# Two-layer Mamba, expert, global and local attention kernel: a new instruction order from a corrected table-load charge, and one exponential a block with a VectorE sum in the last two pairs

## The chip, the cores and the metric

The kernel runs on one core of a Trainium2 chip. The metric is the device time of one execution in microseconds (us), as the median of several runs; lower is better.

## The reference, cut to what matters

The input is `x` of shape (16, 256, 128). Layer 0 adds a Mamba block and a mixture of experts to the normalized input; layer 1 adds two things to it: a global attention and two layers of a local (windowed) attention with a feed-forward part. The change touches the global attention, and, through the order, everything else. Its core is:

```python
q, k, v = _l2norm(q), _l2norm(k), v           # 16 heads of 8
cos = einsum('bhsd,bhtd->bhst', q, k)
g_dist = arccos(clip(cos, -1 + 1e-7, 1 - 1e-7))
attn_score = (1.0 + g_dist) ** (-3.2)
n_r = sum(attn_score, axis=-1)
n_c = sum(attn_score, axis=-2)
k_tilde = n_r ** -1 * attn_score * n_c ** -1
probs = k_tilde / maximum(sum(k_tilde, axis=-1), 1e-12)
out = einsum('bhst,bhtd->bhsd', probs, v)
```

## The kernel before, in words

The 16 sequences of 256 tokens go in 8 pairs (numbers 0 to 7). All work is cut into units: `e_*` are those of the experts (early in the program), `m_*` those of the Mamba scan, `f_*` the normalization between the layers, `g_*` the global attention, and the names in `LAYER` (shift, qkv, norm, heads, score, pt, rsum, pv, on, wo, ln, up, gelu, hid, down) the local attention and its feed-forward part, two layers for each sequence of a pair. A unit has one to four stages, each on one engine.

**What sets the order.** Nothing is left to chance at run time: `schedule()` (from L449) simulates the program on the host before the kernel is built, with a table of durations (`STAGES`, `durations`), a constant `LOAD_TIME` of 1.29 for a change of ScalarE's function table, and for each unit a wanted time. The wanted times come from a rough layout of the pairs plus two tables of offsets, `LATER` (one number for a kind of unit) and `STREAM` (one for each pair of each kind of work). At each moment an engine takes, of the units that are ready, the one with the smallest wanted time; on ScalarE, a unit that needs another table than the loaded one counts 127 later. The result is one list of units for each of TensorE, ScalarE, VectorE, GpSimd and SyncE, and the engines run these lists in order, waiting on semaphores for each other. So a change of the tables changes the order on every engine, and nothing that is computed.

**Table changes.** Ln and Exp share one table, Tanh and Arctan (`g_tan`) need the sigmoid table, Gelu and Silu have their own; Tanh alone is also run with the gelu or silu table. `use()` (L840 to L846, the load is L844) issues one load where the loaded table isn't among those that serve. The planner charges a `g_tan` that comes from the Ln and Exp table with two loads (L529), the kernel issues one there.

**The global attention.** For each sequence of a pair the 16 heads are done in 4 blocks of 4 heads, so a pair has 8 blocks. Block m works in the buffers `cl[m % 2]` and `la[m % 2]`, each 128 x 2048 in SBUF (4 heads, 2 halves of the keys, 256 queries), and `vt[m % 2]`:

- `g_score`: TensorE makes the cosines (L1093), VectorE clips them into `cl` (L1652)
- `g_ln`: ScalarE takes two logarithms (L1390, L1392); `g_sub`: GpSimd subtracts them (L1855)
- `g_tan`: Tanh and Arctan (L1398, L1401), each one instruction of 128 x 2048
- `g_pow`: one Ln of 128 x 2048 (L1408), then eight Exp of 128 x 256 (L1413), one for each head and half, each of which also adds its own row up and writes the sum to `vt` (the profile shows the read of the accumulator as an instruction of its own at L1413)
- `g_av`: VectorE takes the reciprocal of these sums (L1661) and scales the values (L1664), TensorE multiplies (L1107); after every second block ScalarE copies the product (L1422)

The logarithm of block m + 2 waits for the product and for the scaled values of block m, as they use the same buffers. A unit of the local attention that VectorE shares with these is the negated maximum of its scores (L1729); its qkv unit sums squares with a reduction of 128 x 1024 to 128 x 16 (L1704); ScalarE's exponential there is L1465, its copy of q and k L1457, and its square of q and k L1439.

Of the kernel before, what the change touches and what calls it, by code (L numbers as in the profile page):

```python
# [6 lines left out]
ALU = mybir.AluOpType  # L7
ACT = mybir.ActivationFunctionType
AX = mybir.AxisListType
# [25 lines left out]
GH, GD = 16, 8  # L35
HB = 4
# [46 lines left out]
LOAD_TIME = 1.29  # L83
# [6 lines left out]
         "norm": "ln", "pt": "ln", "rsum": "ln", "ln": "ln", "m_in": "silu", "g_tan": "tan", "gelu": "gelu"}  # L90
SWITCH = 127.0

LATER = {"down": 17.13, "e_down": 0.92, "e_lg": -1373.3, "e_ln": 621.99, "e_load": -1698.97, "e_place": -129.783, "e_pre": 351.489,
         "e_route": 144.702, "e_scat": 829.618, "e_store": -223.789, "e_tr": -184.595, "e_up": 44.242, "e_xn": -28.591, "e_xt": -830.714,
         "f_ln": 818.98, "f_tr": -1660.36, "f_xn": -118.536, "f_yg": -111.816, "g_av": 89.144, "g_avT": -202.085, "g_ev": -784.392,
         "g_hd": -35.958, "g_ln": 938.103, "g_norm": -59.145, "g_oT": 238.89, "g_out": 718.35, "g_pow": 876.48, "g_qkv": 45.815,
         "g_score": 49.652, "g_sq": 72.566, "g_sub": 570.978, "g_tan": 44.449, "gelu": -343.785, "heads": 43.677, "hid": -127.469,
         "l_weights": 625.975, "ln": -124.928, "ln2": 1.634, "lnT": -15.963, "m_B": -153.424, "m_C": 17.261, "m_bx": 50.752,
         "m_dt": 18.917, "m_du": 21.175, "m_ex": -16.259, "m_fin": 74.245, "m_hc": 137.244, "m_in": -23.847, "m_load": -295.604,
         "m_out": -935.123, "m_scan": 731.575, "m_sum": 14.942, "m_turn": -247.837, "m_weights": -173.243, "m_xp": 895.808,  # L100
         "norm": -15.561, "on": -140.182, "out": 284.565, "pt": -39.622, "pv": 82.873, "qkv": 47.209, "qn": -65.566, "rsum": -2.347,
         "score": -4.24, "shift": -70.641, "up": -71.786, "wo": 25.239, "x_load": 44.744}

STREAM = {("-", 0): 147.932, ("e", 0): -62.078, ("e", 1): 166.105, ("e", 2): -162.027, ("e", 3): 122.427, ("e", 4): 496.972, ("e", 5): -233.745,
# [14 lines left out]

LOADED = [15.0, 24.0]  # L120

# [7 lines left out]


BY_HALF = 2


def step_of(n, k):
# [30 lines left out]
def durations(unit):  # L165
    u, n, b, k = unit
    if u == "e_xt" and n >= GJ[1]:
        return [("PE", 0.11), ("DVE", 0.22)]
    if u == "e_up" and n >= GJ[1]:
        return [("PE", 0.89), ("DVE", 0.82)]  # L170
    if u == "m_in":
        return [("PE", 0.86), ("ACT", 0.62)] if k % 2 else [("PE", 0.86), ("DVE", 3.15), ("ACT", 0.62)]
    if u == "e_scat":
        return [("POOL", 1.5 * TT * (GP[n + 1] - GP[n]))]
    if u == "qkv":
        return [("PE", 0.86), ("ACT", 0.6)] if k % 3 else [("PE", 1.72), ("ACT", 1.02), ("DVE", 3.6), ("POOL", 2.36)]
    return STAGES[u]
# [253 lines left out]
def schedule():  # L431
# [13 lines left out]
    table = "ln"  # L445
# [50 lines left out]
    while done < todo:  # L496
        for x in [y for y in waiting if y[0] <= now]:
            waiting.remove(x)
            offer(x[1], 0, now)
        again = True  # L500
        while again:
            again = False
            for e in engines:
                if free_at[e] > now:
                    continue
                best = None
                for x in engines[e]:
                    unit, stage, _ = x
                    if not may(unit, stage):
                        continue  # L510
                    needs = NEEDS.get(unit[0]) if e == "ACT" else None
                    cost = want[unit] + (SWITCH if needs and needs != table else 0)
                    if best is None or cost < best[0]:
                        best = (cost, x, needs)
                if best is None:
                    continue
                unit, stage, _ = x = best[1]
                engines[e].remove(x)
                taken.update(holds(unit)[0].get(stage, []))
                needs_banks = takes_banks(unit)  # L520
                if needs_banks and needs_banks[0] == stage:
                    banks[bank_of(unit)] = choose(unit, needs_banks[1])
                    for m, z in enumerate(banks[bank_of(unit)]):
                        idle.remove(z)
                        before_it[bank_of(unit), m] = held_by.get(z)
                        held_by[z] = (bank_of(unit), m)
                takes = stages(unit)[stage][1]
                if best[2] and best[2] != table:
                    takes += LOAD_TIME * (2 if best[2] == "tan" and table == "ln" else 1)  # L529
                    table = best[2]  # L530
                if e == "DVE" and unit[0] in DUAL:
                    takes += max(0.0, pool_until - now)
                    dual_until = now + takes
                if e == "POOL" and unit[0] in POOLED:
                    takes += max(0.0, dual_until - now)
                    pool_until = now + takes
                free_at[e] = now + takes
                plan[e].append(unit)
                line(unit, e).pop(0)
                events.append((now + takes + lands(unit, e), done, unit, stage))  # L540
                done += 1
                again = True
        times = [x for x in free_at.values() if x > now] + [x[0] for x in events + waiting]
        if not times:
            raise ValueError([(e, x[:3]) for e, x in engines.items()])
        now = min(times)
        for x in sorted(y for y in events if y[0] <= now):
            events.remove(x)
            finish(x[2], x[3], x[0])
# [31 lines left out]
def build(nc, d, out):  # L581
    ctx = ExitStack()
    with ctx:
# [160 lines left out]
        for x_, y_ in ((a0, a0), (a2, a3)):  # L744
            q = len(wE)
# [525 lines left out]
        def scalar_program():  # L1271
            for u, i, b, k in order(plan, "ACT"):
# [130 lines left out]
                elif u == "g_pow":  # L1403
# [3 lines left out]
                    a.wait_ge(a_own, arctan_done[m])  # L1407
                    a.activation(at, at, ACT.Ln, bias=one_b[:, 1:2], scale=-2.0).then_inc(a_own, na.up())  # L1408
                    a.wait_ge(a_own, na.n)
                    for hi in range(HB):  # L1410
                        for kt in range(2):
                            part = at[:, hi, kt * L:(kt + 1) * L]
                            e = a.activation(part, part, ACT.Exp, scale=-3.2, accum_out=vt[m % 2][:, kt, hi, GD + 2:GD + 3])  # L1413
# [74 lines left out]
        def vector_program():  # L1488
            for u, i, b, k in order(plan, "DVE"):
# [164 lines left out]
                elif u == "g_av":  # L1654
# [3 lines left out]
                    if m >= 2:  # L1658
                        v.wait_ge(p_av, m - 1)
                    w = vt[m % 2]  # L1660
                    v.reciprocal(w[:, :, :, GD], w[:, :, :, GD + 2]).then_inc(v_own, nv.up())  # L1661
                    v.wait_ge(v_own, nv.n)
                    for kt in range(2):
# [374 lines left out]
```

## Time and profile before

| | us |
|---|---|
| median of 3 runs (2258.05 to 2261.52) | 2261.49 |
| the profiled execution | 2262.57 |
| its span, first to last instruction | 2261.3 |
| busy: PE, DVE, ACT, POOL | 1788.6, 1697.8, 1739.7, 541.0 |

The profile is that of one execution. PE is TensorE, PEld its weight loads, DVE VectorE, ACT ScalarE, POOL GpSimd, SP SyncE. A group of instructions is named by its line in the kernel; "ACT_TABLE_LOAD" at L844 is a load of ScalarE's table. The chain of waits is followed back from the last instruction, at each step to what released it, and ends where it can't be followed; here it covers the span from 1908 us on.

### The profile page before, as it was taken

Reading aid. Unit: us, or ns where it says so; the run is one execution under the profiler, and the core shown is the slowest. Engines: PE = TensorE matmul, PEld = TensorE weight load, DVE = VectorE, ACT = ScalarE, POOL = GpSimd, SP = SyncE. Lnnn points to the kernel's source line nnn. Section 1 sums busy time; section 2 is a strip of 40 time slices with the busy share of each in tenths; the row PEclk is TensorE's granted clock in tenths of the full one; section 3 lists DMA queues with packets and bytes.
Section 4 is the critical chain, followed back from the end, with each engine's and each line's share of the span. In section 5 each row is a group of like instructions: output and inputs, shape, how many; then the busy total and the mean of one; then the engine's idle time right before and its main releaser. Section 6 shows DMA issues by size and latency. Waiting matters only on the chain. (4 is left out here: it accounts for less than half of the span.)

```text
span 2261.3 us, 40539 instructions
## 1 busy us (share of the span) xinstructions
PE 1788.6 (79%) x15282; PEld 1293.3 (57%) x15282; DVE 1697.8 (75%) x2517; ACT 1739.7 (77%) x2887; POOL 541.0 (24%) x270
## 2 busy tenths in 40 slices
PE   3668788998778977788688887886778786779787
PEld 2654566776466654555465565554556464556565
DVE  4878887775999698859976889749984799655552
ACT  2435786857888697887878988977589958887996
POOL 2231122222311222312232222302142121232230
PEclk9687778999889888898788887998988888889888
DMA  6751214350341133114310233013300242000000
GB/s 227 237 170 48 71 38 135 117 147 18 127 136 52 53 117 108 43 39 131 113 39 14 73 122 103 10 49 121 130 21 2 84 141 84 1 1 2 6 1 6
DMA packets 81651, 177.39 MB, mean 78 GB/s; under 512 B 10388, under 2 KB 41940, under 8 KB 81332
## 3 DMA queue, kind: packets, MB, share of 16 engines
q1 hardware_dynamic: 75632, 163.53, 22.4%
q0 software_dynamic: 2816, 7.21, 1.0%
q10 hardware_dynamic: 3012, 4.06, 0.5%
q8 instruction: 125, 2.05, 0.4%
q14 instruction: 66, 0.54, 0.1%
HBM read 161.92 MB, written 12.85 MB: 77 GB/s over the span
## 5 line engine op out<-in xcount | busy, mean ns | idle before, releaser
L1855 POOL TENSOR_TENSOR arena<-arena 128x1024 f32<-128x1024 f32 x128 | 316.3, 2493 | 622.8 <-ACT arena L1392 622.6
L1859 POOL TENSOR_TENSOR arena<-arena,rb 128x1024 f32<-128x1024 f32 x64 | 152.2, 2378 | 866.5 <-DVE rb L1711 866.5
L1579 DVE TENSOR_TENSOR_SCAN ps<-dA,ps 128x1024 f32<-128x1024 f32 x128 | 291.0, 2284 | 1.6 <-ACT dA L1351 1.0
L1153 PE MATMUL ps<-w_l_wqkv,arena 128*128 128x512 f32 x384 | 205.8, 670 | 23.0 <-DVE hB L1587 6.4
L844 ACT ACT_TABLE_LOAD x153 | 196.3, 1283 | 19.3 <-issue 16.6
L1413 ACT ACTIVATE arena<-arena 128x256 f32<-128x256 f32 x512 | 205.3, 402 | 2.0
L1351 ACT ACTIVATE dA<-mv,w_A_log 128x510 f32<-128x510 f32 x256 | 167.8, 711 | 42.2 <-DVE ps L1579 39.1
L1093 PE MATMUL ps<-gqT,gkT 8*128 8x256 f32 x1024 | 164.7, 460 | 38.9 <-DVE arena L1652 16.1
L1652 DVE TENSOR_SCALAR arena<-ps 128x1024 f32<-128x1024 f32 x128 | 155.0, 1217 | 51.3 <-PE ps L1093 50.7
L1573 DVE TENSOR_TENSOR ps<-BC,mv 128x1024 f32<-128x1024 f32 x128 | 181.6, 1425 | 12.9 <-ACT arena L1457 4.1
L849 PE MATMUL ps<-w_ident,arena 128*128 128x128 f32 x623 | 112.1, 326 | 99.5 <-DVE arena L1512 28.6
L1043 PE MATMUL ps<-w_ident,hB 128*128 128x128 f32 x1024 | 162.4, 312 | 28.7 <-DVE hB L1587 28.6
L1043 PEld LDWEIGHTS ps<-w_ident,hB 128*128 128x128 f32 x1024 | 136.5, 162 | 54.4 <-DVE hB L1587 33.2
L1729 DVE TENSOR_REDUCE nmx<-ps 128x4 f32<-128x512 f32 x128 | 87.8, 686 | 97.8 <-PE ps L1181 97.2
L849 PEld LDWEIGHTS ps<-w_ident,arena 128*128 128x128 f32 x623 | 87.2, 169 | 125.0 <-issue 83.2
L1587 DVE TENSOR_TENSOR hB<-ps,BC 128x1024 f32<-128x1024 f32 x128 | 154.4, 1214 | 4.4 <-PE ps L1043 3.6
L1093 PEld LDWEIGHTS ps<-gqT,gkT 8*128 8x128 f32 x1024 | 101.0, 213 | 80.4 <-issue 70.4
L1192 PE MATMUL ps<-arena 64*128 64x192 f32 (+1 forms) x1024 | 118.5, 352 | 35.1 <-DVE rb L1711 13.9
L1390 ACT ACTIVATE arena<-arena,one_b 128x2048 f32<-128x2048 f32 x64 | 127.7, 1996 | 22.8 <-DVE arena L1652 20.9
L1192 PEld LDWEIGHTS ps<-arena 64*128 64x128 f32 x1024 | 92.5, 207 | 83.8 <-issue 49.9
L1153 PEld LDWEIGHTS ps<-w_l_wqkv,arena 128*128 128x128 f32 x384 | 74.4, 211 | 101.9 <-issue 94.1
L1392 ACT ACTIVATE arena<-arena,one_b 128x2048 f32<-128x2048 f32 x64 | 128.2, 2003 | 2.1
(223 smaller groups left out, 4507.7 us busy)
## 6 DMA issues: line engine op xcount, KB each, us to landing
BC<-bc_d SPq DMA_DIRECT2D x224, 512.0 KB, 4.2
BC<-in_experts SPq DMA_DIRECT2D x16, 514.0 KB
arena<-in_experts SPq DMA_DIRECT2D x15, 514.0 KB
mv<-in_experts SPq DMA_DIRECT2D x15, 514.0 KB, 3.4
arena<-in_x SPq DMA_DIRECT2D x8, 256.0 KB, 4.7
xnT_d<-arena SPq DMA_DIRECT2D x8, 256.0 KB, 3.0
hB<-xnT_d SPq DMA_DIRECT2D x8, 256.0 KB, 2.6
x<-in_x SPq DMA_DIRECT2D x8, 256.0 KB, 5.6
```

The costliest lines, as they stand in the source:

```text
L844: a.preload_act_table_set(names[0])
L849: return t.transpose(out_, in_, ident[0:k, 0:k])
L1043: e = t.matmul(lb()[:, tt * P:(tt + 1) * P], hB[k % 2][:, j, tt * P:(tt + 1) * P], ident, is_transpose=True, start=q == j == tt == 0, stop ...
L1093: e = t.matmul(lb(z)[:, kt * L:(kt + 1) * L], gkT[32 * hi:32 * hi + GD, hb, kt * P:(kt + 1) * P], gqT[32 * hi:32 * hi + GD, hb], start=Tru ...
L1153: e = t.matmul(lb(z), hT1[b][:, tt * P:(tt + 1) * P], w_lqkv[:, l, (w + z) * INNER:(w + z + 1) * INNER], start=True, stop=True)
L1192: t.matmul(lb(z)[:, cols], kT[head_rows(z), k, at:at + P], qT[head_rows(z), k, at:at + cols.stop - cols.start], start=kt == 0, stop=False)
L1351: e = a.activation(dA[k % 2][:, j].rearrange("p (s l) -> p s l", s=2)[:, :, 1:], dtv[:, c].rearrange("p (s l) -> p s l", s=2)[:, :, 1:], A ...
L1413: e = a.activation(part, part, ACT.Exp, scale=-3.2, accum_out=vt[m % 2][:, kt, hi, GD + 2:GD + 3])
L1573: v.tensor_tensor(two_banks(unit), Bb[j % 2], bc(du[:, c:c + 1], [P, NG, T]), ALU.mult).then_inc(v_bx, 1)
L1579: v.tensor_tensor_scan(h_, flat2(dA[k % 2]), h_, 0.0, ALU.mult, ALU.add).then_inc(v_scan, 1)
L1652: v.tensor_scalar(cl[m % 2][:, 2 * (k % 2):2 * (k % 2) + 2], two_banks(unit), -1.0 + 1e-7, 1.0 - 1e-7, ALU.max, ALU.min).then_inc(v_gs, 1)
L1855: g.tensor_tensor(la[m % 2][:, half], la[m % 2][:, half], cl[m % 2][:, half], ALU.subtract).then_inc(g_sub, 1)
```

## The change

Five edits. The numbers of `LATER` and `STREAM` are replaced, all of them, so the order on every engine is another. The planner charges one load for each change of table. A constant `LATE = 6` is added: in pairs 6 and 7 `g_pow` issues a single Exp of 128 x 2048 without row sums, and `g_av` on VectorE begins with one reduction that adds up the 256 queries for each key, half and head (2048 elements a partition to 8), with a semaphore wait behind it. The planner's durations for these two units follow. Pairs 0 to 5 keep the eight Exp.

```diff
-LATER = {"down": 17.13, "e_down": 0.92, "e_lg": -1373.3, ...
+LATER = {"down": 21.789, "e_down": -179.804, "e_lg": 315.988, ...
-STREAM = {("-", 0): 147.932, ("e", 0): -62.078, ("e", 1): 166.105, ...
+STREAM = {("-", 0): 145.797, ("e", 0): -176.079, ("e", 1): -91.561, ...
...
 BY_HALF = 2
+LATE = 6
...
+    if u == "g_pow" and n >= LATE:
+        return [("ACT", 4.05)]
+    if u == "g_av" and n >= LATE:
+        return [("DVE", 2.75), ("PE", 1.0)]
...
                 if best[2] and best[2] != table:
-                    takes += LOAD_TIME * (2 if best[2] == "tan" and table == "ln" else 1)
+                    takes += LOAD_TIME
                     table = best[2]
...
                     a.activation(at, at, ACT.Ln, bias=one_b[:, 1:2], scale=-2.0).then_inc(a_own, na.up())
                     a.wait_ge(a_own, na.n)
-                    for hi in range(HB):
+                    if i >= LATE:
+                        e = a.activation(at, at, ACT.Exp, scale=-3.2)
+                    for hi in range(HB if i < LATE else 0):
                         for kt in range(2):
                             part = at[:, hi, kt * L:(kt + 1) * L]
                             e = a.activation(part, part, ACT.Exp, scale=-3.2, accum_out=vt[m % 2][:, kt, hi, GD + 2:GD + 3])
                     e.then_inc(a_at, 1)
...
                     w = vt[m % 2]
+                    if i >= LATE:
+                        v.tensor_reduce(w[:, :, :, GD + 2], la[m % 2].rearrange("p h (k q) -> p k h q", k=2), AX.X, ALU.add).then_inc(v_own, nv.up())
+                        v.wait_ge(v_own, nv.n)
                     v.reciprocal(w[:, :, :, GD], w[:, :, :, GD + 2]).then_inc(v_own, nv.up())
```

Of the wanted times, the ones of the global and local attention and of the scan move little: `g_pow` 876.48 to 816.827, `g_score` 49.652 to 53.464, `score` -4.24 to -2.312, `STREAM` of ("g", 7) -130.691 to -139.982, of ("l", 7) -214.869 to -198.142. The experts' and single others move by hundreds.

## Rows read from the trace of the kernel before

**Rows 1.** The page, part 1: busy time, share of the span and instructions.

```profile
PE 1788.6 (79%) x15282; PEld 1293.3 (57%) x15282; DVE 1697.8 (75%) x2517; ACT 1739.7 (77%) x2887; POOL 541.0 (24%) x270
```

**Rows 2.** Busy time by stretch; columns: length, PE, PEld, DVE, ACT, POOL, clock, DMA.

```profile
1867.00:1940.00 73.00, 50.63 (x440) 35.69 (x444) 59.80 (x73) 65.34 (x120) 16.09 (x7) 0.84 0.20 66
...
1940.00:2262.00 322.00, 257.77 (x2498) 186.38 (x2489) 161.76 (x299) 267.32 (x443) 81.66 (x34) 0.87 0.01 3
```

**Rows 3.** The chain that ended last: shares of the span by engine, then by line.

```profile
PE 6%; ACT 6%; DVE 2%; issue 1%; DVEq 0%; ACTq 0%
...
by line: ACT arena L1413 1.2%; ACT L844 1.1%; issue 1.0%; PE ps L1234 0.8%; PE ps L849 0.8%; ACT arena L1408 0.8%; PE ps L1153 0.7%; ACT arena L1398 0.7%; PE ps L1093 0.5%; ACT arena L1401 0.4%; PE ps L1192 0.4%; PE ps L1107 0.4%; PE ps L12
```

**Rows 4.** Groups of instructions on ACT, whole span.

```profile
L1413 ACT ACTIVATE arena<-arena 128x256 f32<-128x256 f32 x512 | 205.3, 402 | 2.0
...
L1408 ACT ACTIVATE arena<-arena,one_b 128x2048 f32<-128x2048 f32 x64 | 127.5, 1992 | 0.0
...
L1413 ACT ACTIVATION_READ_ACCUMULATOR arena<-arena 128x1 f32 x512 | 95.4, 186 | 0.0
```

**Rows 5.** Groups on ACT from 1867 to 2262 us, where pairs 6 and 7 take powers.

```profile
L1413 ACT ACTIVATE arena<-arena 128x256 f32<-128x256 f32 x128 | 51.3, 402 | 0.5
L844 ACT ACT_TABLE_LOAD x32 | 41.1, 1283 | 0.6
```

**Rows 6.** The chain in order of time; columns: start, length, what.

```profile
1983.00 0.18 ACT arena L1413
1983.19 0.59 ACT arena L1465
...
2143.66 2.19 ACT arena L1413 x11
...
2146.51 1.93 PE ps L1107 x16
...
2227.55 3.31 ACT arena L1413 x16
...
2230.88 0.22 DVE vt L1661
...
2231.67 1.93 PE ps L1107 x16
```

**Rows 7.** Groups of instructions on DVE, whole span: the kernel's reductions.

```profile
L1729 DVE TENSOR_REDUCE nmx<-ps 128x4 f32<-128x512 f32 x128 | 87.8, 686 | 97.8 <-PE ps L1181 97.2
L1704 DVE TENSOR_REDUCE lss<-arena 128x16 f32<-128x1024 f32 x64 | 77.5, 1210 | 53.0 <-ACT arena L1439 52.9
```

**Rows 8.** Waits from 1940 to 2262 us: total, times, longest.

```profile
DVE vt L1661 <- ACT arena L1413: 19.5, 6, 4.5
...
PE ps L1107 <- DVE vt L1664: 3.9, 2, 2.4
```

**Rows 9.** ACT in order of time: first and last of 35 loads straight before Tanh (L1398).

```profile
245.51 1.33 ACT L1351 ACTIVATE dA<-mv,w_A_log 128x510 f32<-128x510 f32 x2 [1.46 <-DVE ps L1579]
246.86 1.28 ACT L844 ACT_TABLE_LOAD   x1
248.15 1.91 ACT L1398 ACTIVATE arena<-arena 128x2048 f32<-128x2048 f32 x1
...
2217.74 0.70 ACT L1465 ACTIVATE arena<-ps 128x640 f32<-128x640 f32 x1
2218.46 1.28 ACT L844 ACT_TABLE_LOAD   x1
2219.76 1.91 ACT L1398 ACTIVATE arena<-arena 128x2048 f32<-128x2048 f32 x1
```

**Rows 10.** The page, part 5: all table loads.

```profile
L844 ACT ACT_TABLE_LOAD x153 | 196.3, 1283 | 19.3 <-issue 16.6
```

**Rows 11.** L844 in two stretches of 180 us; columns: length, ACT busy, clock, DMA.

```profile
820.00:1000.00 180.00, 19.25 (x15) 0.89 0.18 61
1000.00:1180.00 180.00, 10.26 (x8) 0.85 0.30 98
```

More of the change, by code:

```diff
@@ L91 @@
 SWITCH = 127.0
[L93 to L102, printed above, removed]
@@ L104 @@
-STREAM = {("-", 0): 147.932, ("e", 0): -62.078, ("e", 1): 166.105, ("e", 2): -162.027, ("e", 3): 122.427, ("e", 4): 496.972, ("e", 5): -233.745,
[14 rows of a table removed]
+LATER = {"down": 21.789, "e_down": -179.804, "e_lg": 315.988, "e_ln": 174.252, "e_load": -80.536, "e_place": -412.31, "e_pre": 197.091,
+         "e_route": -422.17, "e_scat": 75.416, "e_store": 746.088, "e_tr": 28.199, "e_up": 22.441, "e_xn": -25.847, "e_xt": -1283.66,
+         "f_ln": 932.194, "f_tr": -415.066, "f_xn": -136.104, "f_yg": 296.043, "g_av": 87.191, "g_avT": -1295.52, "g_ev": -639.753,
+         "g_hd": -34.805, "g_ln": 1296.35, "g_norm": -166.971, "g_oT": 533.127, "g_out": 372.703, "g_pow": 816.827, "g_qkv": 41.118,
+         "g_score": 53.464, "g_sq": 26.042, "g_sub": 80.328, "g_tan": 55.828, "gelu": -375.199, "heads": 50.829, "hid": -644.16,
+         "l_weights": 372.755, "ln": -519.782, "ln2": 3.395, "lnT": -0.939, "m_B": 443.054, "m_C": 126.829, "m_bx": 155.512,
+         "m_dt": 46.846, "m_du": 38.48, "m_ex": -12.305, "m_fin": 234.25, "m_hc": 183.447, "m_in": -28.599, "m_load": 252.041,
+         "m_out": -1249.76, "m_scan": 584.13, "m_sum": 17.216, "m_turn": -660.129, "m_weights": -235.564, "m_xp": 1282.27,
+         "norm": -23.494, "on": -821.145, "out": 329.735, "pt": -24.861, "pv": 81.567, "qkv": 47.234, "qn": -624.114, "rsum": 3.63,
+         "score": -2.312, "shift": -80.128, "up": -44.353, "wo": 27.438, "x_load": -205.723}
@@ L120 @@
+STREAM = {("-", 0): 145.797, ("e", 0): -176.079, ("e", 1): -91.561, ("e", 2): -22.018, ("e", 3): -92.228, ("e", 4): -49.362, ("e", 5): -706.602,
[14 rows of a table added]
 LOADED = [15.0, 24.0]
```

28 rows, old and new, of the table STREAM are left out of this document.

## The prediction

> **What bounds the kernel now.** I read the page's busy shares first. PE, ACT and DVE are all busy for 75 to 79% of the span [rows 1]: no engine is full, and what is lost is lost in hand-overs between three nearly equal engines. So work taken from one engine comes back only in part, and the place decides how much. The power step of pairs 6 and 7 (the last 16 of 64 blocks) lies between 1867 and 2262 us, where 128 of the 512 small Exp stand [rows 5]. Next, busy time by stretch: from 1867 to 1940 us DVE is busy 59.80 of 73.00 us beside ACT's 65.34; the Mamba scan still runs there. From 1940 us on, DVE is busy only 161.76 of 322.00 us, PE 257.77, ACT 267.32, so ACT is the fullest at 83% [rows 2]. That is where 12 of the 16 blocks lie (96 of the 128 Exp). Last, the chain of waits: of the span PE and ACT have 6% each, DVE 2%, and the line with the largest share is L1413 itself with 1.2%, or 27 us; the table loads have 1.1% [rows 3]. The change works on the two largest single lines of the end.
>
> **The change, part by part.** The sum is made against the profiled execution, 2262.57 us (span 2261.3 and 1.27 around it); it lies 1.08 above the median, 2261.49, so 1.08 comes off at the end.
>
> Part 1, **the single Exp.** Eight Exp with their reads of the accumulator take 3.31 us in a row [rows 6]; 8 x 0.402 + 8 x 0.186 would be 4.70, so the reads mostly overlap the next Exp [rows 4], and only the stretch in the chain is a fair price. One instruction of 128 x 2048 without a pointer for its bias takes 1.91 us [rows 9], with one 1.99 [rows 4]. The new Exp has none, so 1.91 and a saving of 1.40 a block (1.32 if it is the other). For 16 blocks: 22.4 us of ACT, 16.8 of them after 1940 us.
>
> Part 2, **the reduction.** The kernel has reductions of 512 and 1024 elements a partition, 0.686 and 1.210 us [rows 7]. The step is 0.524 for 512 more, so 2048 takes 1.210 + 2 x 0.524 = 2.26 us. The bounds are 2.26 and 4 x 0.686 = 2.74; the larger row is the nearer, and it reads SBUF as the new one does, so 2.26. For 16 blocks 36.2 us of DVE. It starts when the whole Exp is done, as the reciprocal L1661 did, so the path from the Ln's end to the first product L1107 grows by 2.26 - 1.40 = 0.86 us a block, and 0.05 for the wait. Before, reciprocal and scaling took from 2230.88 to 2231.67 [rows 6]. Room on DVE: 13.20 us idle up to 1940, 160.24 after [rows 2]. The four early blocks ask for 9.0 of the 13.2: no room worth the name. The twelve late ones ask for 27.1 of 160.24. Behind the waiting g_av on DVE stand the clip L1652, the maximum L1729 and the local layers' other steps; TensorE waits for these, and the logarithm of the block after next waits for the product and the values. DVE already waits at L1661 for L1413 six times after 1940, 19.5 us in all; with the Exp 1.40 earlier that shrinks by up to 8 us, which pays for part of the reduction [rows 8].
>
> What of this is on the path? L1413's 27 us in the chain are 27 / 3.31 = 8.2 blocks. Most of these go on with other ACT work, as at 1983.00 to 1983.19; two go over to the product, at 2143.66 and at 2227.55 [rows 6]. The first kind gains 1.40, the second loses 0.91: 6.2 x 1.40 - 2 x 0.91 = 6.9 us. That is the low bound, since other blocks are off this chain only by a little. The high bound is all 22.4. Between them: the tail as a share of ACT's load, 16.8 x 0.83 = 13.9, nothing for the four early blocks, where DVE's 9.0 us more stand against ACT's 5.6 less, and about 2 off for the two hand-overs. I take **-12**. If the cover of DVE's idle time were gone, each reduction would cost its full 2.26.
>
> Part 3, **the planner's charge.** 35 of the 153 loads stand straight before Tanh after work of the Ln and Exp table, at 246.86 the first and at 2218.46 the last [rows 9, 10]. Before, each was charged twice, 35 x 1.29 = 45 us of ScalarE time that the plan held and the chip never spent. The chip didn't pay it, so removing it saves nothing by itself. What it can bring is an order in which the other engines' work is ready when ScalarE really is.
>
> Part 4, **the new order.** The trace can't price an order that it doesn't hold. The bounds come from the table loads: two stretches of 180 us have 15 and 8 loads, 19.25 and 10.26 us [rows 11]; the mean is 153 x 180 / 2261 = 12.2. If all the kernel were like the sparser, 4.2 x 12.6 = 53 fewer loads, 68 us of ACT; like the denser, 2.8 x 12.6 = 35 more, 45 us. By ACT's share of the chain, 6 of 15, that is -27 to +18. Neither end is likely: the last pairs already stand at 32 loads for 16 blocks, 2.0 a block against 153 / 64 = 2.4 for the whole [rows 5, 10]. The wanted times that place scan, scores and powers barely move, so the large layout stays, and experts, whose numbers move by hundreds, come early beside other work. I take **-4**, some eight loads fewer or as much idle time, as a plan with the right charge should fit better than one with 45 us too many; there is no row for more. The SyncE and GpSimd queues are reordered too: POOL is busy 24% [rows 1], and a DMA issued later would show as a wait of DVE or PE in the scan. I cost it at nothing, covered by the prefetch of two buffers; without the cover it would be a few us a pair and is inside the bounds.
>
> Weighed against a rule: before and after the loads ACT loses 0.02 us or less: 245.51 + 1.33 = 246.84, load at 246.86, done at 248.14, Tanh at 248.15; the same at 2218.46 [rows 9]. So a switch costs 1.30 here, and a single charge of 1.29 is right. The Trainium skill, "ScalarE: Activation LUTs", section "What ACT_TABLE_LOAD costs", has every switch at about 2.66 us, a load of 1.28 and a drain of 1.38; the load agrees, the drain isn't seen in these rows. By the page the old double charge of 2.58 would be the right one and the repair a mistake.
>
> Sum: -12 - 4 = -16; 2262.57 - 16 = 2246.6, less 1.08 is **2245.5 us**.
>
> **The rivals.** (A) The forecast, 0.52: 2245, own range 2230 to 2256.
> (B) The order is worth more, 0.12: the loads fall toward the sparser stretch and half of the 27 comes; 2261.5 - 12 - 16 = about 2233 and below, down to 2220. For it: 35 double charges spread over the whole kernel, and 40 us and more of each engine idle in every 180. Against: hand-overs and not loads hold most of that.
> (C) No change, 0.17: PE, 80% busy in the tail and with as much of the chain as ACT, closes the gap; only the 6.9 of the low bound comes, and 4 are lost in a less lucky order; 2258.6.
> (D) Slower by the reduction, 0.10: the product waits for it in most blocks, because the local layers' steps stand before g_av in DVE's new list or because PE has nothing else. A block whose product is on the path loses 0.91; all 16 on it: 14.6, 2276. The others gain 12 / 14 = 0.86 each by my sum (two of 16 hand over today), so it decides from 0.91 n = 0.86 (16 - n), eight blocks. For it: those two in the chain [rows 6]. Against: PE waited only twice, 3.9 us, for the scaled values [rows 8], and DVE is idle for half of the tail.
> (E) Slower by more loads, 0.07: a cheaper charge lets the plan switch oftener. Toward the denser stretch, 35 more, +18 against -12: 2267.5. It decides from 12 / (1.30 x 0.4) = 23 more loads.
> (F) The repair is a mistake, 0.02: if a switch had a cost as long again as the load itself, the plan would now be short by 45 us of ScalarE time and the others' work early and in the way; by the share of 0.4 +18, less 12: 2267.5. This is what the page's 2.66 us comes to. The rows with 0.02 us on both sides of a load leave it little.
> That the new order doesn't do what it is planned for is in C and E.
>
> **How the numbers follow.** The likeliest case gives 2245.5. Range 2223 to 2269: it holds A and C whole, most of B, and of the slow cases what isn't near the bound of D; some 2 in 10 stay out. About 0.2% (4.5 us) is what a measurement of this kernel can tell from none. Faster, below 2257: A, B and a little less, 0.63. Same: most of C and the edge of A, 0.18. Slower, above 2266: D, E, F, 0.19.
>
> **What would show it.** Part 1: at L1413 384 small Exp and 16 of 128 x 2048 at 1.91 us. Part 2: 16 reductions of 128 x 2048 at about 2.26 us on DVE, and L1661 waiting for ACT less than 19.5 us in the tail. Part 3 and 4: table loads near 145 instead of 153, still with 0.02 us before and after; ACT busy about 1707 in place of 1739.7 and DVE about 1734. The end of the scan (L1579) should stay within some us of where it is, with the gain after it. The forecast is wrong if PE's waits at L1107 for the scaled values or at L1093 grow by over 10 us in the tail, if the loads rise, or if the time before 1867 us changes by more than 10 us either way: then the order, and not the single Exp, made the result.

## The result and the profile after

The changed kernel takes 2191.56 us (median of 4 runs, 2180.23 to 2203.48) against 2261.27 for the kernel before on the same chip; the ratio is 0.9696, 95% interval 0.9643 to 0.9748. That is 70 us or 3.0% less, against 16 forecast, and under the range's low end of 2223. The profiled execution took 2192.96 us, its span 2191.6.

The page of the changed kernel, part 1 and the first line of part 4 (as rows 1 and 3 of before):

```profile
PE 1763.4 (80%) x15282; PEld 1279.0 (58%) x15282; DVE 1729.8 (79%) x2533; ACT 1712.0 (78%) x2644; POOL 536.2 (24%) x270
...
PE 6%; ACT 3%; DVE 2%; issue 2%; DVEq 0%; ACTq 0%
```

The busy times are the forecast ones: ACT 1712.0 (forecast 1707, before 1739.7), DVE 1729.8 (forecast 1734, before 1697.8) [rows 1]. The work is what it was said to be, yet the span is 70 us shorter. So the gain is mostly idle time that is gone, on every engine. ACT and DVE together have even a little more to do than before (3441.8 against 3437.5). PE did the same 15282 matmuls in 25 us less, at a mean granted clock of 0.870 against 0.863. The clock doesn't make the gain: where both kernels ran beside each other (e9 below), the kernel before took 2259.20 us at 0.869, and the changed one 2188.44 at 0.870.

Groups of the changed kernel on DVE and ACT: the reduction, the single Exp, the small Exp that are left, the table loads:

```profile
L1669 DVE TENSOR_REDUCE vt<-arena 128x8 f32<-128x2048 f32 x16 | 36.4, 2278 | 9.7 <-ACT arena L1416 9.7
```

```profile
L1420 ACT ACTIVATE arena<-arena 128x256 f32<-128x256 f32 x384 | 154.0, 402 | 1.5
...
L1416 ACT ACTIVATE arena<-arena 128x2048 f32<-128x2048 f32 x16 | 30.6, 1911 | 0.5
```

```profile
L849 ACT ACT_TABLE_LOAD x150 | 192.4, 1283 | 17.2 <-issue 14.5
```

The reduction takes 2.278 us where 2.26 was worked out [rows 7], the Exp 1.911. The loads are 150, three fewer than the 153 of [rows 10].

The time comes from the order, and shows in how much is done by the end of the scan. The scan's last instruction begins at 1910.7 us before and at 1913.2 after. Busy time up to its end and behind it; columns as in rows 2. The kernel before:

```profile
0.00:1913.40 1913.40, 1508.99 (x12620) 1093.12 (x12620) 1521.32 (x2200) 1452.64 (x2399) 453.58 (x234) 0.86 0.29 92
1913.40:2261.40 348.00, 279.58 (x2662) 200.21 (x2662) 176.48 (x318) 287.08 (x488) 87.41 (x36) 0.86 0.01 3
```

The changed kernel:

```profile
0.00:1915.40 1915.40, 1533.23 (x13022) 1114.30 (x13022) 1552.04 (x2258) 1512.54 (x2424) 475.29 (x244) 0.87 0.28 92
1915.40:2191.70 276.30, 230.13 (x2260) 164.65 (x2260) 177.80 (x277) 199.50 (x221) 60.91 (x26) 0.88 0.01 3
```

In the same 1914 us the changed order gets 60 us more of ACT's work and 402 more of PE's matmuls done beside the scan. What is left for the end, where DVE has little to do, falls from 348 to 276 us. ACT's own saving behind the scan can't make that: it is at most 16 x 1.40 = 22 us in all. An order can gain at another place, too: e7 below does it by an earlier end of the scan.

### The profile page after: what moved, and what is told of

The parts are those of the page before. It is cut to its first block and busy times, and to the rows that moved or that the text cites. A ratio compares the mean times of both kernels' runs of the same rounds, so it can differ in the third digit from the quotient of the medians.

```text
span 2191.6 us, 40312 instructions
## 1 busy us (share of the span) xinstructions
PE 1763.4 (80%) x15282; PEld 1279.0 (58%) x15282; DVE 1729.8 (79%) x2533; ACT 1712.0 (78%) x2644; POOL 536.2 (24%) x270
## 5 line engine op out<-in xcount | busy, mean ns | idle before, releaser
L1580 DVE TENSOR_TENSOR ps<-BC,mv 128x1024 f32<-128x1024 f32 x128 | 188.4, 1477 | 8.1 <-ACT arena L1472 1.9
L1420 ACT ACTIVATE arena<-arena 128x256 f32<-128x256 f32 x384 | 154.0, 402 | 1.5
```

The costliest lines, as they stand in the source:

```text
L1580: v.tensor_tensor(two_banks(unit), Bb[j % 2], bc(du[:, c:c + 1], [P, NG, T]), ALU.mult).then_inc(v_bx, 1)
```

## The experiments

All ratios are to the kernel before, run beside each kernel on the same chip. The experiments ran in three groups, and its median differed between them: 2244.4 us for e1 to e4, 2250.7 for e5 to e8, 2265.0 for e9 to e12. The first expectations are in us beside the 2261 of the first result; where a median and a ratio say different things, the ratio counts.

### The four corners: which part made it

**e1_exps_old_order.** The kernel before, every engine's list as it was; the planner isn't touched.

```diff
+LATE = 6
...
-                    for hi in range(HB):
+                    if i >= LATE:
+                        e = a.activation(at, at, ACT.Exp, scale=-3.2)
+                    for hi in range(HB if i < LATE else 0):
...
+                    if i >= LATE:
+                        v.tensor_reduce(w[:, :, :, GD + 2], la[m % 2].rearrange("p h (k q) -> p k h q", k=2), AX.X, ALU.add).then_inc(v_own, nv.up())
+                        v.wait_ge(v_own, nv.n)
```

> The kernel before, every engine's order as it was, and in pairs 6 and 7 the single Exp and the VectorE reduction alone. Theory 1 (the result is the new order's, about five sixths of the 70 us; the single Exp gives what the prediction summed): 12 us less, so 2243 to 2256. Theory 2 (the single Exp opened up the tail, as it frees ScalarE where it is fullest, and gives the larger part): 2190 to 2225. Slower than 2262 would show the reduction on the path of the products (rival D).

Measured: 2259.58 against 2244.36 us, ratio 1.0061 (1.0031 to 1.0091). The single Exp alone makes the old order **slower**, by 0.6%, or 14 us. Neither theory forecast that; rival D did, with 14.6 us for the case that every block's product waits for the reduction. The chain of waits of this kernel, in order of time, shows one:

```profile
1970.20 1.92 ACT arena L1412
...
1972.14 2.30 DVE vt L1665
...
1974.46 0.22 DVE vt L1667
...
1975.26 1.93 PE ps L1108 x16
```

The Exp ends at 1972.12, the reduction (L1665 here) at 1974.44, and the product follows. In the kernel before the chain at this place stayed on ACT and went on with its next work. But the chain, followed from 1894 us on, holds only four of the 14 reductions that begin there, the one above and these:

```profile
2101.72 2.29 DVE vt L1665
...
2188.78 2.30 DVE vt L1665
...
2232.52 2.30 DVE vt L1665
```

Two of the four are of D's kind, from the Exp to the product: at 1972 and at 2232 us. The one at 2188 also starts when the Exp ends, but the chain goes on with other work of DVE, a sum of squares (L1710). The one at 2101 comes behind other work of DVE and holds up more of it, so its whole 2.29 us is on the path. By these four the estimate is 3 x 0.91 + 2.29 = 5.0 us. PE's direct wait for the scaled values behind the scan, 3.9 us before [rows 8], grew to 6.9 only:

```profile
PE ps L1108 <- DVE vt L1670: 6.9, 2, 3.9
```

So the 14 us agree with the number of case D, all 16 blocks on the path, but not with its count. Some of the 14 may be a lower granted clock: at the same 0.867 this kernel took 2254.74 and 2254.88 us, the kernel before 2246.30 and 2249.89, about 7 apart. Why the clock was lower isn't shown.

**e2_new_order_eight_exps.** The changed kernel's lists on every engine, planned with its durations; only the issued instructions go back.

```diff
-                    if i >= LATE:
-                        e = a.activation(at, at, ACT.Exp, scale=-3.2)
-                    for hi in range(HB if i < LATE else 0):
+                    for hi in range(HB):
...
-                    if i >= LATE:
-                        v.tensor_reduce(...)
-                        v.wait_ge(v_own, nv.n)
```

> The changed kernel's order on every engine, planned with its own durations, but with the eight small Exp and no reduction in all pairs. Theory 1: most of the gain stays, 2195 to 2212. Theory 2: most of it goes, 2235 to 2262. With the run of the old order and the single Exp this gives all four corners, so also whether the two parts add up.

Measured: 2176.43 us, 0.969 (0.9635 to 0.9746). The whole gain stays without the single Exp. The result is the order's.

**e3_charge_alone.** The kernel before with its old wanted times and eight Exp:

```diff
-                    takes += LOAD_TIME * (2 if best[2] == "tan" and table == "ln" else 1)
+                    takes += LOAD_TIME
```

> The kernel before with its own wanted times and eight Exp, only the planner's charge for Ln table to Tanh is one load. Theory 1a (the right charge itself makes the better order, the wanted times are secondary): 2190 to 2225. Theory 1b (the order is good because its wanted times were chosen together with the charge; the charge on times that were chosen for another one only disturbs): 2250 or more.

Measured: 2168.56 us, 0.968 (0.9618 to 0.9741). This one line gives as much as the whole change. It even has more table loads than the kernel before:

```profile
L844 ACT ACT_TABLE_LOAD x155 | 198.9, 1283 | 19.8 <-issue 17.0
```

155 against 153, and 72 us less by the ratio (76 by the medians). The number of loads, by which the prediction bounded the order, is not where an order's worth lies.

**e4_new_times_old_charge.** The changed kernel with that line turned back.

```diff
-                    takes += LOAD_TIME
+                    takes += LOAD_TIME * (2 if best[2] == "tan" and table == "ln" else 1)
```

> The changed kernel with its wanted times and single Exp, but the planner charges two loads again for Ln table to Tanh. Theory 1a (charge): 2240 to 2262, the gain is lost. If the wanted times alone carried it: 2195 to 2215. Slower than 2262 would say that any plan made with a charge that its times were not chosen for is bad (1b).

Measured: 2257.97 us, 1.006 (1.0038 to 1.0083). The new wanted times with the old charge give nothing, and 0.6% is lost. Theory 1a has e3 and this run in its ranges. That this kernel is even slower than the one before was the sign of 1b, which e3 refutes. So the pair says that the charge decides, and not why.

### Why the charge matters: true durations, or the ones the times were chosen for

Two theories were left. P: a plan with true ScalarE time fits the chip better. S: the wanted times were chosen for the planner with exactly one load, and with any other durations the same numbers give an ordinary order.

**e5_charge_1_1** and **e6_charge_0_9**: the kernel before, the factor 2 replaced by 1.1 or by 0.9.

```diff
-                    takes += LOAD_TIME * (2 if best[2] == "tan" and table == "ln" else 1)
+                    takes += LOAD_TIME * (1.1 if best[2] == "tan" and table == "ln" else 1)
```

> The kernel before, only the planner charges 1.1 loads for Ln table to Tanh (too much by 0.13 us a time, some 4.5 us over the program, against 45 for two loads). Theory P (the order got better because the plan's ScalarE time became true): nearly all of the gain of the single charge stays, ratio to before 0.968 to 0.975. Theory S (the wanted times were chosen for the planner with exactly one load; any other durations give an ordinary order): most of the gain goes, ratio 0.985 to 1.005.

> The same with 0.9 loads, too little by 0.13 us a time. Theory P: 0.968 to 0.975. Theory S: 0.985 to 1.005. A ratio under 0.97 for one of the two and not for the other would mean that orders scatter by more than the charge explains.

Measured: with 1.1, 2247.33 us, 0.9994 (0.9975 to 1.0012); with 0.9, 2218.38 us, 0.9877 (0.9841 to 0.9913). A charge that is wrong by 0.13 us a time loses all of the gain on one side and more than half on the other. P falls, and both ratios lie where S had them. The traces of e3 and e5 show the same picture as above. The last scan instruction begins within 2 us of the same time with a charge of 1 (e3) and of 1.1 (e5); the stretch before it and the rest:

e3, charge 1:

```profile
1350.00:1866.00 516.00, 427.88 (x3866) 304.92 (x3865) 428.11 (x571) 461.74 (x744) 136.82 (x61) 0.89 0.22 74
1866.00:2160.00 294.00, 241.10 (x2444) 174.02 (x2442) 160.74 (x293) 250.50 (x431) 73.04 (x31) 0.91 0.01 3
```

e5, charge 1.1:

```profile
1350.00:1867.00 517.00, 410.58 (x3579) 288.54 (x3577) 421.77 (x543) 414.31 (x674) 119.98 (x54) 0.87 0.23 75
1867.00:2246.00 379.00, 287.66 (x2805) 207.94 (x2804) 185.96 (x330) 308.42 (x505) 90.71 (x38) 0.86 0.01 3
```

With 1.1 the scan isn't slower, but ACT does 47 us less beside it in the last 517 us, and 58 more remain for the end, which is 85 us longer. Both kernels have 155 table loads. Against the kernel before, whose scan ended at 1913 us, both end it over 45 us earlier; with 1.1 the longer end, 379 us against 348, takes most of that back.

**e7_searched_for_two.** The test from the other side: the wrong charge, but times chosen for it.

```diff
-LATER = {"down": 21.789, ...
+LATER = {...
-STREAM = {("-", 0): 145.797, ...
+STREAM = {...
...
-                    takes += LOAD_TIME
+                    takes += LOAD_TIME * (2 if best[2] == "tan" and table == "ln" else 1)
```

> The changed kernel, but the planner charges two loads, and its wanted times were chosen anew for that charge, by a random search of 1500 s (some 9200 plans) for the shortest plan, from the changed kernel's times. Theory P (a charge of what the chip doesn't pay spoils the order): 0.99 or more. Theory S (the wanted times have to be chosen for the charge that is used, whichever it is): 0.968 to 0.985, most of the gain, though the charge is wrong.

Measured: 2193.19 us, 0.9767 (0.9732 to 0.9802). With the charge as wrong as in the kernel before, 25 minutes of choosing the times for it bring 2.3% against before and 2.9% against e4, the same charge with times for another. Most of the gain is had without any repair. Whether the remaining 0.8% against the changed kernel is the wrong charge or the short search isn't settled.

This kernel gains at another place. Its last scan instruction begins at 1834.8 us, 76 earlier than before, and what is left behind it takes as long as the 348 us of the kernel before:

```profile
1838.00:2189.90 351.90, 285.25 (x2776) 208.23 (x2776) 220.80 (x340) 269.98 (x283) 84.71 (x36) 0.86 0.01 3
```

**Where the plan itself ends.** `schedule()` needs no chip. Run on the host from each kernel as it is, it ends its simulated program at these times:

| kernel | charge, wanted times | plan ends, us | measured ratio |
|---|---|---|---|
| before | 2, old | 2248.4 | 1 |
| e3 | 1, old | 2132.3 | 0.968 |
| changed | 1, new | 2126.3 | 0.9696 |
| e4 | 2, new | 2247.4 | 1.006 |
| e5 | 1.1, old | 2214.2 | 0.9994 |
| e6 | 0.9, old | 2227.1 | 0.9877 |
| e7 | 2, searched for it | 2189.9 | 0.9767 |

This shows S inside the planner. Going from a charge of 1 to 1.1 adds 35 x 0.13 = 4.6 us of ScalarE time to the plan with the old times, and the plan gets 82 us longer; going to 0.9 takes such an amount away, and it gets 95 us longer. The old times make a short plan at a charge of one and at none of the three others, the new ones at one and not at two. The chip follows the plan in direction, and in about six tenths of the size for the two kernels with a single charge (116 and 122 us less planned, about 70 measured); for small differences it doesn't, as e5 and e6 stand the other way round.

### What the single Exp is worth

**e8_single_exp_all_pairs.** The changed kernel's lists, the single Exp and the reduction in all pairs.

```diff
-                    if i >= LATE:
+                    if i >= 0:
                         e = a.activation(at, at, ACT.Exp, scale=-3.2)
-                    for hi in range(HB if i < LATE else 0):
+                    for hi in range(0):
...
-                    if i >= LATE:
+                    if i >= 0:
                         v.tensor_reduce(...)
```

> The changed kernel's order on every engine, with the single Exp and the reduction in all eight pairs, not in the last two alone: 84 us less on ScalarE than with eight small ones everywhere, 146 more on VectorE. If what ScalarE saves counts while the scan runs: under 0.965. If VectorE is the tight engine there, as its busy shares say: slower than the changed kernel by 20 to 60 us, 0.98 to 1.0. The same as the changed kernel (0.965 to 0.973) would say that both hide.

Measured: 2283.08 us, 1.0148 (1.0117 to 1.018), in the direction expected, but more than the 60 us that I had as the end. The changed kernel didn't run in this group; against its ratio in the two others, 0.969 to 0.9696, that is 0.0455 x 2250.66 = 102 us for 48 blocks more, 2.1 us a block. The page's busy times and the reduction:

```profile
PE 1790.9 (78%) x15282; PEld 1298.1 (57%) x15282; DVE 1849.4 (81%) x2581; ACT 1648.8 (72%) x1924; POOL 536.9 (24%) x270
```

```profile
L1669 DVE TENSOR_REDUCE vt<-arena x64: 2252/2277/2289, 272.6 to 2259.9; 128x8 f32<-128x2048 f32 x64
```

ACT has 63 us less to do than in the changed kernel and nothing of that is seen. The loss lies before the end of the scan, whose last instruction began at 1913.2 us in the changed kernel:

```profile
L1586 DVE TENSOR_TENSOR_SCAN ps<-dA,ps x128: 2261/2284/2296, 63.3 to 2008.4; 128x1024 f32<-128x1024 f32 x128
```

It begins 95 us later. What stands behind it takes 273 us against 276. So while the scan runs, a reduction costs nearly its whole 2.28 us and not the 0.86 by which it lengthens its block's path. That is the size of DVE's own time, though DVE is busy for only 81% of the span. PE's direct wait for the scaled values in the whole kernel grows from 14.0 to 40.2 us, which is 26 of the 102. Part of it may be the order, which wasn't planned for this; that wasn't tried.

**e9 to e12, together on one chip, five rounds each.** The changed kernel again; e2 again; e3 again; and the changed kernel with `i >= LATE + 1`, so that only pair 7 has the single Exp.

> The changed kernel once more, unchanged, beside the next three on the same chip. Ratio to before 0.968 to 0.973. It is the base for them.

> The changed kernel's order with the eight small Exp in all pairs, once more. Theory 1 (the single Exp gives the 12 us of the prediction in the new order): 0.004 to 0.008 above the changed kernel. Theory R (what ScalarE saves, the reduction takes back, as in the old order): the same within 0.002, or below the changed kernel.

> The kernel before with the single charge alone, once more. Theory S: the changed kernel's new wanted times add little or nothing over the old ones under the charge for which these were chosen, so within 0.003 of the changed kernel, on either side. If the retuned times were worth something beside the charge: over 0.004 above the changed kernel.

> The changed kernel's order, the single Exp and the reduction in pair 7 alone, all of whose blocks come when the scan is over. If the reduction costs only where the scan fills VectorE and the Exp's saving counts behind it: 0.002 to 0.005 below both the changed kernel and the one with eight Exp. If the reduction stands on the way of the products in the tail too: the same as the one with eight Exp or above it.

| kernel | us | ratio (95%) |
|---|---|---|
| e9: changed | 2188.5 | 0.969 (0.9662 to 0.9719) |
| e10: its order, eight Exp | 2183.8 | 0.966 (0.9632 to 0.9689) |
| e11: before, charge alone | 2193.0 | 0.9691 (0.966 to 0.9722) |
| e12: single Exp in pair 7 alone | 2183.7 | 0.9653 (0.962 to 0.9687) |

All four intervals overlap. In the new order the single Exp gives nothing that can be measured: e10 is below e9, not 0.004 to 0.008 above as 12 us would be. That it costs something isn't shown either, as e10's runs had the higher granted clock (0.872 to 0.876 against 0.870 to 0.873), and at 0.872 e9 took 2185.33 and 2196.77 us, e10 2195.28. That pair 7 alone is better than none or both isn't shown either; e12 is 0.0037 under e9, which touches the 0.002 to 0.005 that was expected, but it equals e10. The retuned times add nothing that can be measured over the old ones under one load.

## Why the prediction was wrong

The forecast was 16 us less, 12 by the single Exp and 4 by the order. Measured, the order gives about 70 (e2, e3) and the single Exp nothing. So both terms were wrong, and the range was missed by the second.

- **Part 1, right.** 16 Exp of 1.911 us, as worked out.
- **Part 2, right in size, wrong in place.** 2.278 us against 2.26, and room on DVE after the scan. But I took -12 for both parts on the chip. The old order gives +14 (e1), the new one nothing that can be measured (e9, e10). The step that failed here is "the tail as a share of ACT's load, 16.8 x 0.83": it priced the saving by how busy ACT is, and the reduction at nothing but "about 2 off" because DVE is idle there. What the runs show in its place: in the old order four reductions stand in the last chain, three with the longer path that the text had and one with its whole time (e1). With all 64 blocks it is 2.1 us a block, near the "full 2.26" of the text for the case without cover (e8). That e1's +14 is also 16 x 0.86 is a match of numbers. How the saving of ScalarE is lost in the new order is open.
- **Part 3, the fact right, the conclusion wrong.** The 35 double charges were there, and a switch costs 1.30 us: in the changed kernel too, the loads are 1.283. But "the chip didn't pay it, so removing it saves nothing by itself" looked at the 45 us alone. A charge in the planner isn't a cost that is saved, it is an input of every later choice. The one line is worth 72 us by the ratio (e3, and again in e11: 70).
- **Part 4, the step that made the forecast wrong.** It took -4 for the new order, bounded by -27 and +18, from the number of table loads, when the real one is about -70 (e2: 0.969 without the single Exp). Three loads fewer, or two more, go with it. "The wanted times barely move, so the large layout stays" was read as small effect. It should have been read the other way: the g and l times barely moved although the charge did, so they fit the single charge already, and it was the double charge that didn't fit them. With e3 and e4 and the ends of the plans this is shown. No row of the trace could give the size. The bound that it gives for a reorder of the whole program is the idle time of the engines, 21 to 25% of the span, and the tail in which DVE is half idle. The planner, though, could be asked: it puts the changed kernel 122 us before the old one. "There is no row for more" stopped at the trace.
- **Rival B** had the direction and the place of the argument (35 charges over the kernel, 40 us idle of each engine in every 180), with 0.12 and a floor of 2220; its half of 27 is 13.5, where its sum took 16. Its mechanism, fewer loads, isn't what happened. **Rival F**, that the repair is a mistake, falls: the charge of 2 is 3% slower with the old times. By e7 that says nothing of what a switch really takes, since a plan with the double charge can be nearly as good. What it takes is told by the 0.02 us on both sides of a load [rows 9]. The 2.66 us that the Trainium skill, "ScalarE: Activation LUTs", section "What ACT_TABLE_LOAD costs", gives for every switch isn't what this kernel's loads took, and the measurement decides.
- **Where the gain lies**: I had put down, as a sign that the order made the result, a change of over 10 us in the time before 1867 us. The scan's end stays within 3 us and doesn't show that sign, though the order did make the result: up to it 60 us more of ACT's work are done. The other signs stayed quiet too: the loads fell to 150, DVE waited for the Exp 9.7 us in the tail and PE for the scaled values 2.1. They watched the single Exp and the loads, and not the order.

## What to carry to other kernels

When an order comes from a planner whose weights were tuned, the weights belong to the exact durations of that planner: change one duration by 0.13 us without choosing the weights anew and 3% can go, and a wrong duration with weights chosen for it does most of what the right one does. So before a change to such a planner is judged from a trace, ask the planner how long its own plan is with and without it, and run a change of instructions in the old order and the new order without it. An instruction put between two engines can cost by the longer path of its chain, or by its engine's time where that engine's work is what others wait for; that an engine is idle for a fifth of the span (DVE in e8) covers neither.

## What the runs showed of the hardware that I had not expected

The same kernel on two chips gave medians 24 us apart (charge alone: 2168.56 and 2193.01, the kernel before beside it 2244.36 and 2264.99), while the ratios, 0.968 and 0.9691, agree. The granted clock doesn't explain it: at the same 0.876 one run took 2168.68 us on the first chip, another 2201.71 on the second. Most of the difference of the two profiled executions lies before the end of the scan, whose last instruction began at 1862.8 us in one and at 1894.8 in the other; why is open. Within one group of runs the clock and the time do go together: the kernel before took 2236.33 us at 0.875 and 2258.87 at 0.861. Only ratios taken on one chip could carry differences of 0.5% here.
